# TensorE's loop body turned by one phase: H of the next step inside both sides of the branch, and T(31) behind the loop

## What is computed

```
e = stack([tbl_f[ids[:, f]] for f in range(32)], axis=1)         # (512, 32, 64)
h = inp = e
for i, (W, b) in enumerate(((W0, b0), (W1, b1), (W2, b2))):      # 128 outputs each
    nxt = einsum('bjk,bzk,ojz->bok', h, inp, W.reshape(128, -1, 32)) + b[None, :, None]
    h, o = nxt[:, :64], nxt[:, 64:]        # the last layer keeps all 128 as o
    outs.append(o)
z = sum(concatenate(outs, axis=1), axis=2)                       # (512, 320)
h = maximum(concatenate([z, dense_ctx], axis=1) @ W_top1 + b_top1, 0)
h = maximum(h @ W_top2 + b_top2, 0)
y = h @ W_top3
```

## Time and profile before

| what | value |
|---|---|
| median of 3 runs | 660.75 us (659.64 to 661.15) |
| the profiled execution | 659.79 us |
| its span | 658.1 us |
| TensorE busy (matmul) | 626.3 us, 95% |
| weight loads | 520.0 us |
| VectorE busy | 483.4 us, 73% |
| ScalarE busy | 214.7 us, 33% |
| GpSimd busy | 128.6 us, 20% |
| mean granted TensorE clock | 0.982 |

### The profile page before, as it was taken

How to read it: one execution, slowest core, us unless ns; L and a number is a source line. 1 busy time by engine, 2 the same in 40 slices (tenths; PEclk the granted TensorE clock), 3 DMA queues, 4 the chain that set the end, 5 groups by cost and what they waited for, 6 DMA issues and landing times.

```text
span 658.1 us, 32257 instructions
## 1 busy us (share of the span) xinstructions
PE 626.3 (95%) x14488; PEld 520.0 (79%) x14488; DVE 483.4 (73%) x497; ACT 214.7 (33%) x354; POOL 128.6 (20%) x137
## 2 busy tenths in 40 slices
PE   6844999999999999999999999999999999999998
PEld 6843778888888888888888888888888888888773
DVE  4538778888888888888888888888888888841000
ACT  2421444334433444323233323233333333332012
POOL 7765234444445444000000000000000000000000
PEclk9886999999999999999999999999999999999999
DMA  5110011111111111000000000000000000011000
GB/s 182 30 29 19 20 27 26 28 29 28 27 21 27 30 28 26 13 13 13 12 12 12 12 12 12 12 12 12 12 12 12 12 12 12 12 29 54 11 1 0
DMA packets 31658, 14.87 MB, mean 23 GB/s; under 512 B 24177, under 2 KB 28897, under 8 KB 31378
## 3 DMA queue, kind: packets, MB, share of 16 engines
q1 hardware_dynamic: 27442, 10.26, 7.3%
q0 software_dynamic: 4192, 4.25, 2.9%
HBM read 8.03 MB, written 0.00 MB: 12 GB/s over the span
## 4 chain that ended last, share of the span: by engine, by line
PE 90%; POOL 5%; issue 2%; DVE 1%; DMA 1%; ACT 0%; POOLq 0%; DVEq 0%; ACTq 0%
PE psT L440 20%; PE psX L383 20%; PE psT L464 8%; PE psT L450 7%; PE psT L424 7%; PE psT L427 6%; POOL G_sb L249 5%; PE psX L427 5%; PE psX L424 4%; PE psX L394 3%; PE psX L511 2%; PE psX L403 1%; PE psT L525 1%; PE psX L541 1%; PE psX L283 1%
## 5 line engine op out<-in xcount | busy, mean ns | idle before, releaser
L440 PE MATMUL psT<-T_sb,W1d 64*64 64x256 f32 x1024 | 234.3, 379 | 0.0
L444 PE MATMUL psT<-T_sb,W1d 64*64 64x256 f32 x1024 | 234.3, 379 | 0.0
L450 PE MATMUL psT<-T_sb,W1d 64*64 64x256 f32 (+3 forms) x2048 | 205.3, 300 | 0.0
L730 DVE TENSOR_TENSOR prod<-X 128x1024 f32 (+3 forms) x208 | 171.2, 891 | 17.3 <-PE psT L427 17.1
L767 DVE STREAM_TRANSPOSE PT<-prod 128x4608 f32<-128x4608 f32 x31 | 154.0, 4968 | 0.0
L440 PEld LDWEIGHTS psT<-T_sb,W1d 64*64 64x64 f32 x1024 | 131.3, 133 | 27.8 <-issue 14.4
L464 PE MATMUL psT<-T_sb,W1d 64*64 64x64 f32 (+2 forms) x1536 | 141.7, 270 | 0.0
L444 PEld LDWEIGHTS psT<-T_sb,W1d 64*64 64x64 f32 x1024 | 131.3, 133 | 0.0
L383 PE MATMUL psX<-PT,W0T 32*64 32x256 f32 x4464 | 128.5, 377 | 2.7 <-issue 2.5
L383 PEld LDWEIGHTS psX<-PT,W0T 32*64 32x64 f32 x4464 | 113.8, 131 | 20.5 <-issue 19.0
L450 PEld LDWEIGHTS psT<-T_sb,W1d 64*64 64x64 f32 x2048 | 123.6, 133 | 0.8
(11 more groups left out here) (86 smaller groups left out, 559.2 us busy)
## 6 DMA issues: line engine op xcount, KB each, us to landing
X<-T_sb SPq DMA_DIRECT2D x64, 64.0 KB, 2.0
kept<-grams SPq DMA_DIRECT2D x128, 16.5 KB
G_sb<-in_L_rec_W SPq DMA_DIRECT2D x2, 1024.0 KB, 6.6
E_q<-in_tbl,ids_g POOLq DMA_INDIRECT x96
prod<-in_W_top SPq DMA_DIRECT2D x2, 512.0 KB, 3.5
G_sb<-in_L_rec_W SPq DMA_DIRECT2D x1, 512.0 KB, 5.7
G_sb<-in_tbl,ids POOLq DMA_INDIRECT x32, 2.4
dT<-dT SPq DMA_DIRECT2D x3, 32.0 KB, 3.1
```

The source lines that it names most:

```text
L440: mm(psT[low, 0, 0:HF * SMP], W1d[low, HF + k, :], cross.rearrange("p v (z y) s -> p v z y s", y=HF)[:, :, :, k, :], start=start, stop=sto ...
L444: mm(psT[high, 0, 0:HF * SMP], W1d[low, k, :], T_flat[low, SMP * row:SMP * (row + HF)], start=start, stop=stop, tile_position=(0, C))
L450: last = mm(out[:, SMP * 4 * a:], W1d[high, HF * v + k, :], T_flat[high, SMP * (row + 4 * a):SMP * (row + HF)], start=start, stop=stop and ...
L730: return tt(out, x[:, :, z0:z0 + nz].unsqueeze(3).broadcast_to(shape), x[:, :, y0:y0 + ny].unsqueeze(2).broadcast_to(shape), ALU.mult)
```

## The change

H(n+1) with its wait is moved into both sides of the branch, behind T(n), and a body now begins with the branch for step n. The order of matmuls is the same as before: T(n), H(n+1), g2(n), ..., T(n+1). What moves is where the jump back and the branch stand between them. H is written twice in each loop. T(0) comes into the first loop, and g0(31) and T(31) stand behind the second without a branch.

```diff
             def tower_in_turn(n):
+                pe.wait_ge(px_ready, n + 1)
+                pe.wait_ge(ht_ready, n + 1)
                 turn = pe.snap(n % 2)
                 with pe.If(turn < 1):
                     g0_matmuls(n, 0)
                     t_matmuls(n, 0)
+                    pe.wait_ge(t_by_dve, ND * (n + 1))
+                    h_matmuls(n + 1)
                 with pe.Else():
                     g0_matmuls(n, 1)
                     t_matmuls(n, 1)
+                    pe.wait_ge(t_by_dve, ND * (n + 1))
+                    h_matmuls(n + 1)
 
             def step(n, lookups):
-                pe.wait_ge(t_by_dve, ND * (n + 1))
-                h_matmuls(n + 1)
+                tower_in_turn(n)
                 g2_matmuls(n, 0, 4)
                 h_transposes(n + 1)
...
-                pe.wait_ge(px_ready, n + 2)
-                pe.wait_ge(ht_ready, n + 2)
-                tower_in_turn(n + 1)
 
             prologue()
             pe.wait_ge(w_evac, W_BANKS)
-            pe.wait_ge(px_ready, 1)
-            pe.wait_ge(ht_ready, 1)
-            g0_matmuls(0, 0)
-            t_matmuls(0, 0)
             with pe.Fori(0, 2 * LOOKUP_PAIRS) as n:
                 step(n, True)
             with pe.Fori(2 * LOOKUP_PAIRS, STEPS - 1) as n:
                 step(n, False)
+            pe.wait_ge(px_ready, STEPS)
+            pe.wait_ge(ht_ready, STEPS)
+            g0_matmuls(STEPS - 1, 1)
+            t_matmuls(STEPS - 1, 1)
```

## The result

| | before | after |
|---|---|---|
| median of 6 runs each, us | 659.88 (657.46 to 661.15) | 672.27 (671.89 to 674.58) |
| profiled execution, us | 659.79 | 673.15 |
| its span, us | 658.1 | 671.5 |

The ratio is 1.0203, 95% interval 1.0186 to 1.0219: slower, as forecast, but by 12.4 us where 6.8 were forecast, and outside the range.

A forecast was written before the change was run, and what follows sets the result against it. TensorE, paced by its own matmuls, was taken as the bound. -2.7 + 9.5 = +6.8 us on the profiled 659.79 us gives 666.6, and 0.96 us more for the median gives 667.5 us; range 662.5 to 671.5.

The forecast's parts named there:

- What bounds: Whole kernel: TensorE is the bound, paced by its own matmuls, which are busy 626.3 us of a 658.1 us span.
- part 1: Between T and H: without branch instructions there, even steps gain 0.18 us and odd ones 0; 2.7 us gained.
- Part 2: Between g2 and g0: the jump back ahead of the branch adds 0.45 us of sequencer time a step; 9.5 us lost.
- the terms: Ahead of g0, time exposed per step: first loop 0.45 us odd, 0.39 even; second loop 0.29 odd, 0.19 even.
- the 0.15 us of T(0): Ahead of step 0: T(0), behind a loop's top and an untaken branch, comes about 0.15 us behind the wait for `H_T`.
- hidden: Between g2 and g0: the jump back is hidden under g2 and costs nothing; 658.0 us, faster; chance 0.07.
- half of it: Ahead of g0: the sequencer's leads are longer by 0.1 us or the jump is shorter; 664.5 us; chance 0.07.
- the sum 3 us lower: Between g2 and g0: with 108 ns per compare-and-branch, 0.35 us a step is added and the forecast is some 3 us lower.
- Part 3: Between H and g2, even steps: the jump over the odd side fits the sequencer's 0.55 us lead; cost 0, uncovered 5 us.
- First touches move: First entry of the odd sides, steps 1 and 13: up to 1.3 us more or less per loop, 670 us; chance 0.06.

The follow-up runs named there:

- the kernel with H once: Against the changed kernel, H stands once behind the place where both sides meet, the body still beginning with the branch; 666.65 us, ratio to before 1.010.

## Why the prediction was partly right

**What bounds, and part 1: right.** The gain of 0.18 us in each even step and 0 in each odd one is what the trace after shows, H 0.21 or 0.22 us behind the copy in both.

**Part 2: right in kind and size, a little high.** A pair of steps takes 35.39 us in the first loop where it took 34.80, and 33.89 where it took 33.62 in the second. Each pair has one even step; with its 0.18 us of part 1 added back, the jump back costs 0.77 and 0.45 us a pair; the terms were 0.45 + 0.39 = 0.84 and 0.29 + 0.19 = 0.48. (The four terms as listed add up to 9.3 us; the 9.5 of the sum comes out only with the 0.15 us of T(0) in it.) Load and first matmul of g0 start together, as forecast. The rivals "hidden" and "half of it" are thus ruled out, and so is the sum 3 us lower. Parts 1 and 2 in the steady stretches: 5.7 us forecast, 4.6 measured.

**Part 3: right in the steady steps.** H to g2, from first matmul to first matmul, is 4.07 or 4.08 us in the steady steps of both kernels (4.14 once). It is not right in steps 0 and 12: 7.43 and 7.04 us.

**The step that failed** is the price of the loop entries. The sum puts them at nothing, and the rival "First touches move" prices them at "up to 1.3 us more for each loop", with a chance of 0.06 for all stalls of that kind. Measured in the two entry stretches: 4.6 and 4.9 us more, less the 0.7 and 0.3 us that the parts put there, 8.5 us in all. I took the 1.23 us stall of the first touch in the kernel before as the price of a first jump whatever it passes. The runs show two things in its place.

- The stand depends on how far the jump goes: 0.6 us at 40 matmuls in the kernel with H once, 3.3 to 3.7 us at 112 in the changed kernel. A fetch that begins only behind the jump has to be waited for whole; the 1.23 us were the end of one that had begun before.
- A stand of that length can cost again, by the clock: 1.5 us in step 0 and 2.9 us in step 12.

The stands are 3.35 + 2.96 = 6.3 us beyond the usual H to g2, so together that is 10.7 us, against 8.5 + 2.0 us to be explained (2.0 us are the entry stalls of before, 0.7 and 1.3, that went).

The price could have been bounded from the trace of before. The fetch in question begins there at 290.5 us, and weights are loaded again at 293.07 us: 2.6 us for a fetch that is waited for whole, to which the time from the jump to the start of the fetch comes. The bound from both sides that I gave every other unknown was missing here.

By the accounting: 6.8 forecast, - 1.1 for parts 1 and 2, + 8.5 for the entries, - 0.8 up to step 0, which varies as much between executions (61.5 to 65.3 us over the kernels here) and has no cause that I can show: 13.4 us, the difference of the two spans.

**What stays open.** Which code each fetch holds, and so why it begins before one jump and behind another; why the clock falls after some stands of about 3 us and not after others; the extra 0.2 to 0.3 us in the branch of the kernel with H once; and where between 330 and 440 the limit lies.

## What to carry to other kernels

A runtime branch inside a loop has two prices. The steady one is read from the lead of the sequencer at each junction, and a jump belongs where that lead is longest. The other is paid once per loop, when the branch first passes code that hasn't run: keep the sides short (the longest stand of an entry was 0.6 to 2.0 us with 40 matmuls of this kind and 1.9 to 3.8 us with 112), and don't cut loops needlessly. Letting the side that runs first stand first gained 0.27% in one kernel and nothing in two. A stand of TensorE of about 3 us should be priced both ways, with the clock falling behind it (1.5 to 2.9 us more here) and without. And before an entry is compared between two profiles, compare the granted clock of both there.

## What the hardware showed that I had not expected

- The first jump over a side of 112 matmuls that hasn't run took 3719 and 3333 ns, the same jump in a steady step 169 ns.
- Every stand of more than a microsecond in the steps ended 1.3 to 2.1 us after a fetch of 16,384 bytes had landed.
- After stands of 2.84, 2.98 and 3.3 to 3.7 us the granted clock was 0.50 for 3.4 to 6.8 us; after others of 3.10, 3.13 and 3.79 us, and after 2.2 us, it stayed at 1.00.
- A body of some 330 matmuls is fetched once (22 packets), one of 440 again and again (110 packets, 60 us).
- Moving code without changing it put 0.2 to 0.3 us more between two neighbouring sequencer instructions of a branch, in each pass.
